# Turning dequantised weights on TensorE: transpose and separate low-rank sum, or identity product with accumulation

## The chip, the cores and the metric

One NeuronCore of a Trainium2 chip runs the whole program. The metric is the device time of one execution in microseconds. The kernel before has a median of 907.61 us in three runs (907.22 to 911.1).

## The reference, cut to what matters

Two post-norm layers over 4 sequences of 512 tokens, 256 channels. Layer 0 is attention (16 heads, 4 key/value heads, rotary) and a mixture of 8 experts with a shared expert; layer 1 is causal attention and the feed-forward block that the change touches:

```
def dequant4bit(q, scale):
    return (q.astype(jnp.float32) - 7.5) * jnp.repeat(scale, 64, axis=1)
w_up = dequant4bit(w_up_q, w_up_scale).T                      # 256 x 1024
y1 = x1 @ w_up + b_up + x1 @ w_up_lora_a @ w_up_lora_b        # rank 16
x2 = jax.nn.relu(y1)
w_down = dequant4bit(w_down_q, w_down_scale).T                # 1024 x 256
y2 = x2 @ w_down + b_down + x2 @ w_down_lora_a @ w_down_lora_b
```

The kernel folds the low-rank part into the weights: it computes w_up + a_up b_up and w_down + a_down b_down once, in float32, and keeps both in SBUF.

## The kernel before

Each engine has one program in order. Part A is layer 0 up to the shared expert, then a loop runs 23 tiles of 128 tokens through the experts, then part C is layer 1. Part C is driven by a list of steps written out by hand (C_START, C_FIRST and so on). Every engine walks the same list and does its share of each step. A step name is a kind and a number; a plus sign means the next batch; `m` is the next of the 44 row-maximum steps of a batch.

Most steps of TensorE fill one of three PSUM banks ("units"), which go round in the order of the list. `take` waits until the bank used three such steps earlier has been emptied, `filled` waits on the reading engine for TensorE, `consumed` waits until a step's bank has been read.

The steps that matter, all in C_START, with the line of their TensorE part:

- Wb, Wat0 to Wat2 (L608): biases and the low-rank "a" factors are transposed; VectorE copies them out (ua_t, da_t).
- Wu0 to Wu3 (L608): four 128x128 transposes of the dequantised up weight each. ScalarE copies the bank to w_up (L978).
- Wul0 to Wul3 (L616): one product of the 16 rows of ua_t with 512 columns of n_ub. VectorE adds the bank to w_up (L1326).
- Wd0 to Wd3 and Wdl0 to Wdl3 (L608, L616): the same for the down weight, with two products of 256 columns. ScalarE copies (L981), VectorE adds (L1330).
- Wq, Wo (L608): transposes of the layer-1 projections, copied by ScalarE.
- cL0, cL1 (L1335 and the lines after L1065): VectorE adds the gathered expert rows and normalises half a batch each. GpSimd gathers the rows by indirect DMA (L1439), for batch 0 before everything else of part C, for batch b+1 after cL1 of batch b.
- cX0, cX1 (L608): transposes of these halves. cQ, cV (L616): projections. cK: VectorE splits queries and keys into three bfloat16 parts, SyncE stores them to DRAM and loads them back stacked.
- m (L830, L832 on TensorE, L1369 on VectorE): scores for the row maxima and their reduction.

The product lines call `nc.tensor.matmul(out, stationary, moving)`; a float32 product shows as two pairs of a weight load and a matmul record, a transpose as one. The weights w_up and w_dn are first used by the cH and cD steps of batch 0, far behind C_START.

Of the kernel before, what the change touches and what calls it, by code (L numbers as in the profile page):

```python
# [25 lines left out]
ALU = mybir.AluOpType  # L26
# [3 lines left out]
P = 128  # L30
B = 4
S = 512
C = 256
# [14 lines left out]
RANK = 16  # L48
# [28 lines left out]
A_LAST = """.V0 -F3 | | -P0 | -P1 | | .F0 | -N0 | -N1 | -R0 | .F1 | | | | .F2 | | |"""  # L77
A_END = """-F3 =Sg0 =Sg1 -P0 =Sg2 =Sg3 =Su0 -P1 =Su1 =Su2 -N0 =Su3 =D0 -N1 -R0 =D1 RK0 -Sg0 -Sg1
-Sg2 -Sg3 -Su0 -Su1 ID0 -Su2 -Su3 -D0 -D1"""
C_START = """Wb0 Wat0 Wat1 Wat2 Wu0 Wul0 Wu1 Wul1 Wu2 Wul2 Wu3 Wul3 cL0 Wq0 Wq1 Wq2 Wo0 Wd0 Wd1 cX0 cL1 Wd2 Wd3 cX1 cQ0 cQ1 cK0 cQ2  # L80
cK1 cQ3 cK2 cV0 cK3 cV1 Wdl0 Wdl1 +cL0 Wdl2 +cX0 +cL1 Wdl3 +cX1 m +cQ0 m +cK0 m m +cQ1 m m m m +cK1 m m
+cQ2 m m m +cK2 m m +cQ3 m m m m +cK3 m m m m m m m m m m m m m m m m m m m m +cV0 m m m m m cM0 +cV1"""
C_FIRST = """+m | | +m +m | +m | +m +m | .cF0 +m +m +m +m | +m +m +m | +m +m +m +m +m | +m +m +m +m | .cF1 +m +m +m | +m +m | +m
+m +m +m +m | +m +m +m | .cF2 +m +m +m +m +m +m +m +m +m | +cM0 >cL0 | >cL1 |"""
# [15 lines left out]
def expand(names, b, m):  # L100

    steps = []
    for x in names.split():
        sign = x[0] if x[0] in "=-.+>" else ""
        to = b + {"=": -2, "-": -1, ".": 0, "+": 1, ">": 2}[sign] if sign else 0
        x = x[len(sign):]
        if x == "m":
            if to < B:
                steps.append(("max", to, m[0]))
            m[0] += 1  # L110
        elif 0 <= to < B:
            kind = x.rstrip("0123456789")
            steps.append((kind, to, int(x[len(kind):])))
    return steps
# [28 lines left out]
def c_order():  # L143

    return (expand(C_START, 0, [0]) + attention_order([C_FIRST, C_SECOND, C_THIRD, C_LAST], "catt")
            + expand(C_END, B, [0]))


def post_ln_layers(nc, ins, out):
# [4 lines left out]
    with ExitStack() as ctx:  # L154
# [23 lines left out]
        ident = place([P])  # L178
# [102 lines left out]
        w_up = place([NC_, HID])  # L281
        w_dn = place([NK, C])
# [5 lines left out]
        n_up = place([NK, C])  # L288
        n_ups = place([NK, C // BLOCK])
        n_dn = place([2, HID])  # L290
        n_dns = place([2, HID // BLOCK])
        n_ua = place([2, RANK])
        n_ub = place([HID])
        n_da = place([NK, RANK])
        n_db = place([C])
        ua_t = place([C])
        da_t = place([HID])
# [119 lines left out]
        def qk_columns(i):  # L417

            return slice(C, QK0) if i == 0 else slice(P * (i - 1), P * i)
# [7 lines left out]
        def take(pe, step):  # L427

            u = unit_no[step]
            if u >= UNITS:  # L430
                pe.wait_ge(unit_free[u % UNITS], u // UNITS)
            return ps[:, 8 - UNITS + u % UNITS, :]

        def filled(eng, step):

            u = unit_no[step]
            eng.wait_ge(unit_full[u % UNITS], u // UNITS + 1)  # L437
            return ps[:, 8 - UNITS + u % UNITS, :]

        def consumed(eng, step):  # L440

            u = unit_no[step]
            eng.wait_ge(unit_free[u % UNITS], u // UNITS + 1)

        def full_of(step):
            return unit_full[unit_no[step] % UNITS]

        def free_of(step):
            return unit_free[unit_no[step] % UNITS]
# [152 lines left out]
        def _(pe):  # L602
            def transposes(step, pieces):

                dst = take(pe, step)
                for col, src, idn, rows in pieces:
                    n = src.shape[0]
                    last = nc.tensor.transpose(dst[0:rows, col:col + n], src, idn)  # L608
                last.then_inc(full_of(step), 1)

            def products(step, groups):

                dst = take(pe, step)
                for (rows, lo, hi), pairs in groups:
                    for n, (a, w) in enumerate(pairs):
                        last = nc.tensor.matmul(dst[0:rows, lo:hi], a, w, start=(n == 0), stop=(n == len(pairs) - 1))  # L616
                last.then_inc(full_of(step), 1)

            def cols(t):
                return slice(P * t, P * (t + 1))  # L620

            pe.wait_ge(s_ident, 16)
            for step in a_steps:
                n, b, i = step
# [15 lines left out]
                elif n == "attS":  # L640
# [5 lines left out]
                    for g in range(4):  # L646
                        if g % 2 == 0 and head0 * b + i:

                            pe.wait_ge(exp_done[g // 2], head0 * b + i)
                        last = nc.tensor.matmul(ps[:, g, :], k_stack[0:STACK, b % 2, hg, cols(kt)],  # L650
                                                q_stack[0:STACK, b % 2, 4 * hg + g, :], start=True, stop=True)
                        if g % 2:
                            last.then_inc(s_full[g // 2], 1)
                elif n == "attP":
# [6 lines left out]
                    for g in range(4):  # L661
                        if g % 2 == 0:
                            pe.wait_ge(exp_done[g // 2], k + 1)
                        last = nc.tensor.matmul(ps[32 * g:32 * g + 32, 4, :], v_aug[:, kt, hg, :],  # L664
                                                (probs0, probs1)[i % 2][:, g, :], start=(kt == 0), stop=(kt == NT - 1))
# [31 lines left out]
                elif n == "ID":  # L697
                    dst = take(pe, step)
                    for t in range(TT):
                        if t % (TT // 2) == 0:  # L700
                            pe.wait_ge(hot_ready, t // (TT // 2) + 1)
                        last = nc.tensor.matmul(dst[:, 0:48], pos_hot[:, t, :], pick[:, t, :], start=(t == 0),
                                                stop=(t == TT - 1))
# [74 lines left out]
            for step in c_steps:  # L778
                n, b, i = step
# [12 lines left out]
                    transposes(step, [(0, n_b[0:4 + NK, :], ident[0:4 + NK, 0:4 + NK], P)])  # L792
                elif n == "Wu":
                    pe.wait_ge(deq, 1)
                    c, half = i // 2, i % 2
                    transposes(step, [(P * r, n_up[:, 4 * half + r, cols(c)], ident, P) for r in range(4)])
                elif n == "Wul":
                    c, half = i // 2, i % 2
                    consumed(pe, ("Wat", 0, 0))
                    products(step, [((P, 0, 512), [(ua_t[0:RANK, cols(c)], n_ub[0:RANK, 512 * half:512 * half + 512])])])  # L800
                elif n == "Wd":
                    pe.wait_ge(deq, 2)
                    transposes(step, [(P * (2 * r + c), n_dn[:, c, cols(2 * i + r)], ident, P)
                                for r in range(2) for c in range(2)])
                elif n == "Wdl":
                    consumed(pe, ("Wat", 0, 2))
                    products(step, [((P, C * r, C * (r + 1)), [(da_t[0:RANK, cols(2 * i + r)], n_db[0:RANK, :])])
                                    for r in range(2)])
                elif n in ("cX", "cN"):
                    pe.wait_ge(x2_ready if n == "cX" else x3_ready, 2 * b + i + 1)  # L810
                    transposes(step, [(P * (2 * t + c), x_sb[:, NT * b + 2 * i + t, cols(c)], ident, P)
# [10 lines left out]
                elif n == "max":  # L822
# [4 lines left out]
                    dst = take(pe, step)  # L827
                    w = P * (qt + 1)
                    for g in range(nh):
                        nc.tensor.matmul(dst[:, w * g:w * (g + 1)], cq_stack[0:STACK, b % 2, h0 + g, cols(qt)],  # L830
                                         ck_stack[0:STACK, b % 2, h0 + g, 0:w], start=True, stop=True)
                        last = nc.tensor.matmul(dst[:, w * g + P * qt:w * (g + 1)], identb, negmask,  # L832
                                                start=False, stop=True, skip_group_check=True)
                    last.then_inc(full_of(step), 1)
                elif n == "cM":
                    pe.wait_ge(m_parts, b + 1)
                    dst = take(pe, step).bitcast(BF16)
                    for t in range(NT):
                        last = nc.tensor.transpose(dst[0:2 * NH, cols(t)], mparts[:, t, :, :].rearrange("p a h -> p (a h)"),
                                                   identb)  # L840
                    last.then_inc(full_of(step), 1)
                elif n == "cattS":
# [6 lines left out]
                    for g in range(4):  # L849
                        h = 4 * hg + g  # L850
                        if g % 2 == 0:

                            pe.wait_ge(exp_done[g // 2], k)
                        last = nc.tensor.matmul(ps[:, g, P * kt:S], ck_stack[0:STACK + 2, b % 2, h, cols(kt)],  # L854
                                                cq_stack[0:STACK + 2, b % 2, h, P * kt:S], start=True, stop=True)
                        if g % 2:
                            last.then_inc(s_full[g // 2], 1)
                elif n == "cattP":
# [7 lines left out]
                    for g in range(4):  # L866
                        last = nc.tensor.matmul(ps[32 * g:32 * g + 32, 4, P * kt:S],  # L867
                                                cv_aug[:, b % 2, kt, 4 * hg + g, :],
                                                cprobs[:, i % 2, g, P * kt:S], start=(kt == 0), stop=(kt == NT - 1))
# [10 lines left out]
                elif n == "cI":  # L880

                    half, k = i // NK, i % NK
# [156 lines left out]
        def _(v):  # L1039
# [72 lines left out]
            for step in a_steps:  # L1112
                n, b, i = step
# [3 lines left out]
                elif n == "rp":  # L1117
# [12 lines left out]
                    r = rot[:, :, qk_columns(i)].rearrange("p t (d h) -> p t d h", d=HD)  # L1130
# [42 lines left out]
                elif n == "R":  # L1173
# [3 lines left out]
                    for t in range(NT):  # L1177
                        last = nc.vector.max(top8[:, t, :], logits[:, t, :])
# [131 lines left out]
            for step in c_steps:  # L1310
                n, b, i = step
                if n == "Wat":
                    dst = ua_t if i == 0 else da_t[:, 512 * (i - 1):512 * i]
                    w = C if i == 0 else 512
                    nc.vector.tensor_copy(dst[0:RANK, :], filled(v, step)[0:RANK, 0:w]).then_inc(free_of(step), 1)
                elif n == "Wb":
# [2 lines left out]
                    nc.vector.tensor_copy(b_qk, src[:, 0:4]).then_inc(free_of(step), 1)  # L1319
                    consumed(v, step)  # L1320
                    nc.vector.tensor_scalar(b_qk[:, 0:2], b_qk[:, 0:2], 0.25, None, ALU.mult).then_inc(bqk_ready, 1)
                elif n == "Wul":
                    c, half = i // 2, i % 2
                    consumed(v, ("Wu", 0, i))
                    dst = w_up[:, c, 512 * half:512 * half + 512]
                    nc.vector.tensor_tensor(dst, filled(v, step), dst, ALU.add).then_inc(free_of(step), 1)  # L1326
                elif n == "Wdl":
                    consumed(v, ("Wd", 0, i))
                    dst = w_dn[:, 2 * i:2 * i + 2, :].rearrange("p r n -> p (r n)")
                    nc.vector.tensor_tensor(dst, filled(v, step), dst, ALU.add).then_inc(free_of(step), 1)  # L1330
                elif n == "cL":

                    rows = x_sb[:, NT * b + 2 * i:NT * b + 2 * i + 2, :]
# [14 lines left out]
                elif n == "cV":  # L1348
# [5 lines left out]
                    for t in range(2):  # L1354
                        last = nc.vector.tensor_tensor(cv_aug[:, b % 2, 2 * i + t, :, 0:HD], src[:, t, :, :],
                                                       bv_b.rearrange("p (h d) -> p h d", d=HD), ALU.add)
# [31 lines left out]
                elif (n == "cH" and i < 2) or (n == "cI" and i % NK == 0):  # L1388

                    half = i if n == "cH" else i // NK  # L1390
# [131 lines left out]
```

## Time and profile before

| | us |
|---|---|
| median of three runs | 907.61 |
| lowest, highest | 907.22, 911.1 |
| the profiled execution | 910.58 |
| its span, first to last instruction | 908.5 |
| TensorE busy | 798.4 |
| VectorE busy | 490.1 |
| ScalarE busy | 367.3 |
| GpSimd busy | 98.5 |

The mean granted TensorE clock over the span is 0.936 of full speed. "Busy" of TensorE is time with a matmul record open, so it includes the tail of each. PE in a row is TensorE's matmul queue, PEld its weight loads, DVE VectorE, ACT ScalarE, POOL GpSimd. Times in a timeline are from the start of the span; the expert loop ends near 455 us and the attention of layer 1 starts at 551.65 us.

### The profile page before, as it was taken

What the parts mean: (1) busy time and instruction counts of PE and PEld (TensorE: products, weight loads), DVE (VectorE), ACT (ScalarE), POOL (GpSimd) and SP (SyncE); (2) the same over time, 40 slices, a digit from 0 to 9 for tenths busy, and PEclk for the clock granted to TensorE, in tenths of its full rate; (3) what the DMA queues carried; (4) which work ended last, traced back from release to release, by engine and by line L of the source; (5) the groups of instructions that cost most, each with busy time, mean ns of one, the idle gap of its engine ahead of it and who ended that gap; (6) DMA issues with size and microseconds to landing.
All of it is one profiled execution on the core that took longest, in us unless ns stands there. A gap on an engine that the chain in (4) does not pass through costs nothing. (4 is left out here: it accounts for less than half of the span.)

```text
span 908.5 us, 11697 instructions
## 1 busy us (share of the span) xinstructions
PE 798.4 (88%) x3907; PEld 419.0 (46%) x3908; DVE 490.1 (54%) x1369; ACT 367.3 (40%) x581; POOL 98.5 (11%) x111
## 2 busy tenths in 40 slices
PE   5599999999998899999987778878998889979886
PEld 3222435344345456666653333434464445533665
DVE  2743852763645522222265794888665955664363
ACT  3388785875842011111142205534423532146130
POOL 0000000000000111111811101221011101012000
PEclk9699999999999999999978798978999979889999
DMA  6558025024061061111117580007200450000000
GB/s 203 152 189 277 10 85 160 1 82 117 24 205 50 18 183 42 45 46 46 29 49 220 148 234 4 1 25 210 68 1 2 129 173 1 2 1 24 12 12 24
DMA packets 51582, 75.02 MB, mean 83 GB/s; under 512 B 7606, under 2 KB 44762, under 8 KB 49226
## 3 DMA queue, kind: packets, MB, share of 16 engines
q1 hardware_dynamic: 49660, 69.26, 25.3%
q0 software_dynamic: 1872, 5.11, 2.2%
q8 instruction: 29, 0.48, 0.2%
q14 instruction: 21, 0.17, 0.1%
HBM read 46.57 MB, written 27.66 MB: 82 GB/s over the span
## 5 line engine op out<-in xcount | busy, mean ns | idle before, releaser
L616 PE MATMUL ps<-arena 128*128 128x256 f32 (+5 forms) x1084 | 340.8, 464 | 22.4 <-DVE arena L1203 5.0
L616 PEld LDWEIGHTS ps<-arena 128*128 128x128 f32 (+1 forms) x1084 | 206.7, 201 | 118.5 <-issue 75.6
L921 ACT ACTIVATE arena<-ps 128x1024 f32<-128x1024 f32 x128 | 124.2, 1027 | 32.8 <-PE ps L650 32.6
L1016 ACT ACTIVATE arena<-ps 128x1024 f32<-128x1024 f32 (+3 forms) x128 | 83.2, 705 | 94.2 <-PE ps L854 93.9
L1369 DVE TENSOR_REDUCE arena<-ps 128x1 f32<-128x512 f32 (+3 forms) x176 | 101.1, 635 | 35.8 <-PE ps L832 31.8
L721 PE MATMUL ps<-arena 128*128 x184 | 88.0, 602 | 1.2 <-DVE arena L1274 1.2
L830 PE MATMUL ps<-arena 96*128 96x128 bf16 (+3 forms) x256 | 66.4, 316 | 14.6 <-DVE arena L1369 9.4
L608 PE MATMUL ps<-arena 128*128 128x128 f32 (+3 forms) x237 | 42.0, 320 | 41.2 <-DVE arena L1086 17.1
L650 PE MATMUL ps<-arena 96*128 96x512 bf16 x256 | 71.5, 391 | 6.7 <-DMA arena<-q_stacks_dram 3.6
L1456 POOL TENSOR_SCALAR_AFFINE_SELECT arena<-arena 128x512 f32<-128x512 f32 x64 | 43.1, 675 | 286.4 <-ACT arena L1016 286.1
L664 PE MATMUL ps<-arena 128*32 128x512 f32 x512 | 69.7, 612 | 2.9 <-DVE arena L1148 2.7
L1415 POOL DMA_INDIRECT arena<-xs_dram,arena x23 | 21.9, 954 | 409.9 <-DVE arena L1268 303.8
L949 ACT ACTIVATE arena<-ps 128x512 f32<-128x512 f32 x23 | 13.8, 598 | 125.7 <-PE ps L721 125.7
L608 PEld LDWEIGHTS ps<-arena 128*128 128x128 f32 (+3 forms) x237 | 32.6, 161 | 56.0 <-issue 19.9
L854 PE MATMUL ps<-arena 98*128 98x512 bf16 (+3 forms) x256 | 50.1, 315 | 8.0 <-ACT arena L1016 4.8
L650 PEld LDWEIGHTS ps<-arena 96*128 96x128 bf16 x256 | 17.9, 98 | 82.5 <-ACT arena L921 40.7
L867 PE MATMUL ps<-arena 128*32 128x128 f32 (+3 forms) x512 | 50.8, 470 | 0.4 <-POOL arena L1456 0.4
L832 PE MATMUL ps<-arena 128*128 128x128 bf16 x256 | 50.7, 227 | 0.0
L830 PEld LDWEIGHTS ps<-arena 96*128 96x128 bf16 x256 | 25.5, 100 | 47.8 <-DVE arena L1369 31.6
L721 PEld LDWEIGHTS ps<-arena 128*128 128x128 f32 x184 | 33.7, 194 | 26.1 <-issue 25.0
L1095 DVE STREAM_TRANSPOSE arena<-arena 128x512 f32<-128x512 f32 x32 | 22.6, 706 | 41.2 <-ACT arena L928 21.2
L738 PE MATMUL ps<-arena 128*128 x184 | 43.6, 380 | 0.8 <-ACT arena L955 0.8
(144 smaller groups left out, 723.7 us busy)
## 6 DMA issues: line engine op xcount, KB each, us to landing
arena<-stacks_dram SPq DMA_DIRECT2D x16, 768.0 KB, 6.3
arena<-in_gate_up_proj SPq DMA_DIRECT2D x8, 1024.0 KB, 9.5
arena<-q_stacks_dram SPq DMA_DIRECT2D x8, 768.0 KB, 5.9
stacks_dram<-arena SPq DMA_DIRECT2D x16, 384.0 KB, 3.3
arena<-in_down_proj SPq DMA_DIRECT2D x8, 512.0 KB, 8.7
stacks_dram<-arena SPq DMA_DIRECT2D x16, 256.0 KB, 3.6
q_stacks_dram<-arena SPq DMA_DIRECT2D x8, 384.0 KB, 4.1
yg_dram<-arena SPq DMA_DIRECT2D x23, 128.0 KB, 1.7
```

Of the source, the lines that this page charges most:

```text
L608: last = nc.tensor.transpose(dst[0:rows, col:col + n], src, idn)
L616: last = nc.tensor.matmul(dst[0:rows, lo:hi], a, w, start=(n == 0), stop=(n == len(pairs) - 1))
L650: last = nc.tensor.matmul(ps[:, g, :], k_stack[0:STACK, b % 2, hg, cols(kt)], q_stack[0:STACK, b % 2, 4 * hg + g, :], start=True, stop=True)
L664: last = nc.tensor.matmul(ps[32 * g:32 * g + 32, 4, :], v_aug[:, kt, hg, :], (probs0, probs1)[i % 2][:, g, :], start=(kt == 0), stop=(kt = ...
L721: last = nc.tensor.matmul(ps[:, 2 * half + up, :], xg_t[:, half, c, :], gu[:, e, c, FE * up:FE * (up + 1)], start=(c == 0), stop=(c == 1))
L830: nc.tensor.matmul(dst[:, w * g:w * (g + 1)], cq_stack[0:STACK, b % 2, h0 + g, cols(qt)], ck_stack[0:STACK, b % 2, h0 + g, 0:w], start=Tru ...
L832: last = nc.tensor.matmul(dst[:, w * g + P * qt:w * (g + 1)], identb, negmask, start=False, stop=True, skip_group_check=True)
L854: last = nc.tensor.matmul(ps[:, g, P * kt:S], ck_stack[0:STACK + 2, b % 2, h, cols(kt)], cq_stack[0:STACK + 2, b % 2, h, P * kt:S], start= ...
L867: last = nc.tensor.matmul(ps[32 * g:32 * g + 32, 4, P * kt:S], cv_aug[:, b % 2, kt, 4 * hg + g, :], cprobs[:, i % 2, g, P * kt:S], start=( ...
L921: nc.scalar.activation(probs[:, 2 * p:2 * p + 2, :], ps[:, 2 * p:2 * p + 2, :], ACT.Exp)\
L1016: nc.scalar.activation(cprobs[:, i % 2, 2 * p:2 * p + 2, P * kt:S], ps[:, 2 * p:2 * p + 2, P * kt:S], ACT.Exp).then_inc(exp_done[p], 1)
L1369: nc.vector.tensor_reduce(mneg[:, qt, h0:h0 + nh], filled(v, step)[:, 0:nh * w].rearrange("p (h n) -> p h n", n=w), AX.X, ALU.max, negate= ...
```

## The change

For each 128x128 tile of the up and down weights, the transpose becomes an ordinary product with the identity as the moving operand, with the tile as stationary operand as before. Directly behind it the low-rank product for the same 128 columns is accumulated onto the same PSUM columns. ScalarE then copies the finished bank. The steps Wul and Wdl are gone from the list and from both engines. The list is reordered: cL0 comes directly behind Wat2; Wq, Wo, Wu0, Wu1 follow; Wu2 stands between cX0 and cX1 of batch 0; Wu3 and Wd0 behind cV1; Wd1 and Wd2 ahead of cX0 of batch 1 and Wd3 between its cX0 and cX1.

```diff
-C_START = """Wb0 Wat0 Wat1 Wat2 Wu0 Wul0 Wu1 Wul1 Wu2 Wul2 Wu3 Wul3 cL0 Wq0 Wq1 Wq2 Wo0 Wd0 Wd1 cX0 cL1 Wd2 Wd3 cX1 cQ0 cQ1 cK0 cQ2
-cK1 cQ3 cK2 cV0 cK3 cV1 Wdl0 Wdl1 +cL0 Wdl2 +cX0 +cL1 Wdl3 +cX1 m +cQ0 m +cK0 m m +cQ1 m m m m +cK1 m m
+C_START = """Wb0 Wat0 Wat1 Wat2 cL0 Wq0 Wq1 Wq2 Wo0 Wu0 Wu1 cX0 cL1 Wu2 cX1 cQ0 cQ1 cK0 cQ2
+cK1 cQ3 cK2 cV0 cK3 cV1 Wu3 Wd0 +cL0 Wd1 Wd2 +cX0 +cL1 Wd3 +cX1 m +cQ0 m +cK0 m m +cQ1 m m m m +cK1 m m
...
                 elif n == "Wu":
                     pe.wait_ge(deq, 1)
+                    consumed(pe, ("Wat", 0, 0))
                     c, half = i // 2, i % 2
-                    transposes(step, [(P * r, n_up[:, 4 * half + r, cols(c)], ident, P) for r in range(4)])
-                elif n == "Wul":
-                    c, half = i // 2, i % 2
-                    consumed(pe, ("Wat", 0, 0))
-                    products(step, [((P, 0, 512), [(ua_t[0:RANK, cols(c)], n_ub[0:RANK, 512 * half:512 * half + 512])])])
+                    dst = take(pe, step)
+                    for r in range(4):
+                        nc.tensor.matmul(dst[:, cols(r)], n_up[:, 4 * half + r, cols(c)], ident, start=True, stop=True)
+                        last = nc.tensor.matmul(dst[:, cols(r)], ua_t[0:RANK, cols(c)], n_ub[0:RANK, cols(4 * half + r)],
+                                                start=False, stop=True, skip_group_check=True)
+                    last.then_inc(full_of(step), 1)
                 elif n == "Wd":
                     pe.wait_ge(deq, 2)
-                    transposes(step, [(P * (2 * r + c), n_dn[:, c, cols(2 * i + r)], ident, P)
-                                for r in range(2) for c in range(2)])
-                elif n == "Wdl":
+                    consumed(pe, ("Wat", 0, 1))
                     consumed(pe, ("Wat", 0, 2))
-                    products(step, [((P, C * r, C * (r + 1)), [(da_t[0:RANK, cols(2 * i + r)], n_db[0:RANK, :])])
-                                    for r in range(2)])
+                    dst = take(pe, step)
+                    for r in range(2):
+                        for c in range(2):
+                            nc.tensor.matmul(dst[:, cols(2 * r + c)], n_dn[:, c, cols(2 * i + r)], ident, start=True,
+                                             stop=True)
+                            last = nc.tensor.matmul(dst[:, cols(2 * r + c)], da_t[0:RANK, cols(2 * i + r)],
+                                                    n_db[0:RANK, cols(c)], start=False, stop=True, skip_group_check=True)
+                    last.then_inc(full_of(step), 1)
...
-                elif n == "Wul":
-                    c, half = i // 2, i % 2
-                    consumed(v, ("Wu", 0, i))
-                    dst = w_up[:, c, 512 * half:512 * half + 512]
-                    nc.vector.tensor_tensor(dst, filled(v, step), dst, ALU.add).then_inc(free_of(step), 1)
-                elif n == "Wdl":
-                    consumed(v, ("Wd", 0, i))
-                    dst = w_dn[:, 2 * i:2 * i + 2, :].rearrange("p r n -> p (r n)")
-                    nc.vector.tensor_tensor(dst, filled(v, step), dst, ALU.add).then_inc(free_of(step), 1)
```

## Rows read from the trace of the kernel before

**Rows 1.** The page, busy time: us, share of span, instructions.

```profile
PE 798.4 (88%) x3907; PEld 419.0 (46%) x3908; DVE 490.1 (54%) x1369; ACT 367.3 (40%) x581; POOL 98.5 (11%) x111
```

**Rows 2.** Stretches: busy us (records) by engine, granted clock, DMA share, GB/s.

```profile
core 0: us, PE busy (x) PEld busy (x) DVE busy (x) ACT busy (x) POOL busy (x), PEclk, DMA share, GB/s
456.00:460.00 4.00, 4.00 (x22) 2.05 (x19) 2.52 (x6) 1.20 (x2) 1.65 (x2) 1.00 0.51 158
460.00:464.00 4.00, 4.00 (x12) 1.93 (x12) 1.39 (x2) 0.80 (x2) 2.24 (x3) 0.59 0.39 113
464.00:468.00 4.00, 4.00 (x13) 2.50 (x13) 2.06 (x5) 3.19 (x5) 0.00 (x0) 0.50 0.02 8
468.00:472.00 4.00, 3.79 (x22) 3.39 (x21) 3.60 (x17) 2.71 (x6) 0.00 (x0) 0.63 0.00 0
...
492.00:496.00 4.00, 2.57 (x10) 1.95 (x11) 3.86 (x9) 0.00 (x0) 0.00 (x0) 0.85 0.98 242
496.00:500.00 4.00, 1.43 (x4) 0.61 (x2) 3.76 (x14) 0.00 (x0) 0.00 (x0) 0.50 1.04 356
...
508.00:512.00 4.00, 4.00 (x15) 2.26 (x14) 0.74 (x2) 0.60 (x1) 3.09 (x4) 0.51 0.32 84
...
530.00:540.00 10.00, 8.09 (x53) 4.16 (x54) 10.00 (x19) 0.00 (x0) 0.00 (x0) 0.83 0.99 288
```

**Rows 3.** Timeline, GpSimd and VectorE, 461 to 476: start, us, what.

```profile
461.91 0.94 POOL L1439 DMA_INDIRECT arena<-yg_dram,arena  x1 [0.31 <-issue]
...
465.87 0.69 DVE L1326 TENSOR_TENSOR arena<-ps,arena 128x512 f32<-128x512 f32 x1 [2.35 <-PE ps L616]
466.48 0.68 DVE L1335 TENSOR_TENSOR arena<-arena 128x512 f32<-128x512 f32 x1
...
475.66 0.41 DVE L1086 TENSOR_SCALAR arena<-arena 128x256 f32<-128x256 f32 x1
```

**Rows 4.** Timeline of TensorE, 458 to 478.

```profile
458.43 0.66 PE L608 MATMUL ps<-arena 128*128 128x128 f32 x4
...
459.02 1.12 PE L616 MATMUL ps<-arena 16*128 16x512 f32 x2
...
460.07 0.66 PE L608 MATMUL ps<-arena 128*128 128x128 f32 x4
...
462.64 1.11 PE L608 MATMUL ps<-arena 128*128 128x128 f32 x4
...
463.69 2.07 PE L616 MATMUL ps<-arena 16*128 16x512 f32 x2
...
465.69 5.38 PE L608 MATMUL ps<-arena 128*128 128x128 f32 x24
...
471.28 1.53 PE L608 MATMUL ps<-arena 128*128 128x128 f32 x12 [0.21 <-DVE arena L1086]
...
476.12 0.66 PE L608 MATMUL ps<-arena 128*128 128x128 f32 x4 [3.31 <-DVE arena L1086]
...
477.51 10.53 PE L616 MATMUL ps<-arena 128*128 128x512 f32 x24 [0.73 <-ACT arena L993]
```

**Rows 5.** Timeline of TensorE and VectorE, 492 to 510.

```profile
492.11 1.96 PE L616 MATMUL ps<-arena 16*128 16x256 f32 x8 [0.58 <-ACT arena L1006]
...
495.87 1.29 DVE L1330 TENSOR_TENSOR arena<-ps,arena 128x512 f32<-128x512 f32 x2
497.08 0.68 DVE L1335 TENSOR_TENSOR arena<-arena 128x512 f32<-128x512 f32 x1
...
501.88 1.11 PE L608 MATMUL ps<-arena 128*128 128x128 f32 x4 [4.45 <-DVE arena L1086]
...
507.32 1.12 PE L608 MATMUL ps<-arena 128*128 128x128 f32 x4 [2.32 <-DVE arena L1086]
...
509.32 0.69 DVE L1369 TENSOR_REDUCE arena<-ps 128x4 f32<-128x512 f32 x1 [1.28 <-PE ps L832]
```

## The prediction

> **What bounds the kernel now.** I read the page first: TensorE is busy 88% of the span and VectorE 54% [rows 1]. A share says nothing about this change, since its steps all stand between the last expert tile (455 us) and the first score matmuls of layer 1 (551 us). So I took the table of stretches [rows 2], then the timelines. From 530 to 540 us VectorE is busy 10.00 of 10.00 us with the row maxima, whatever TensorE does; what counts is when that run of maxima can start. It starts behind cX1 of batch 1, which TensorE begins at 507.32 us and whose first maximum follows at 509.32 [rows 5]. The question is therefore what moves these 507.32 us. Two chains lead there, one behind the other.
>
> First chain: VectorE adds the fourth Wul at 465.87, starts cL0 at 466.48, and cL0 and cL1 end at 476.07 [rows 3]. cX1 of batch 0 starts then, at 476.12, and the first cQ at 477.51 [rows 4]. Here VectorE is last and TensorE waits for it. Everything up to cV1 hangs on the first cQ through the part splitting and its stores to DRAM.
>
> Second chain: after cV1, VectorE adds Wdl0 and Wdl1 (495.87), begins cL0 of batch 1 at 497.08, lets cX0 go at 501.88, adds Wdl2, does cL1, lets cX1 go at 507.32 [rows 5]. TensorE has little to do meanwhile: 1.43 of the 4.00 us from 496 on, and that at the low clock [rows 2].
>
> **What the change removes.** Eight adds of about 0.69 us on VectorE and the eight products Wul, Wdl with their banks. In the first chain cL0 no longer stands behind Wul3's add, but it needs the four gathers; the last is issued at 461.91 [rows 3] and DMA traffic has died out at 464 (0.39 busy before, 0.02 after) [rows 2], so cL0 could start at about 464.7: 1.8 us earlier. In the second chain cL0 of batch 1 starts at 495.85 in place of 497.08 (1.23), and cL1 follows without Wdl2's add (0.65): 1.9 us. On VectorE alone the change is worth 1.8+1.9 = 3.7 us. The extra ScalarE evacuations are none: it copied the eight turned tiles before too, and now does it in stretches where it is idle. SyncE and GpSimd issue the same things in the same order; the waits on the turned low-rank tiles, which Wu and Wd now hold, are met before 458 us, well ahead of any of these steps.
>
> **What it adds to TensorE.** A transpose leaves one record, a float32 product two (Wul: x2 for one product) [rows 4]. The price of a record of 128 columns: twelve transposes take 1.53 us and four 0.66, so 0.109 us at the high clock; twenty-four take 5.38 and four 1.11, so 0.2135 us at the low clock [rows 4]. 512 columns are four times that (0.436 and 0.854), and the row count doesn't matter: eight 16-row records of 256 columns need 1.96 us, as 8 x 0.218 and the tail of the last say [rows 5].
>
> Each new step has four pieces, a 128-row product with the identity and a 16-row product, two records of 128 columns each. Columns alone make that 4 x 0.109 = 0.44 us a piece at the high clock and 0.85 at the low one. But a piece goes from 128 stationary rows to 16 and back, and the trace prices that. Between the starts of Wu2 and Wu1 lie 460.07-458.43 = 1.64 us, with 4 x 0.109 + 2 x 0.436 = 1.31 us of columns: 0.33 us for one change to 16 rows and one back. At the low clock it is 465.69-462.64 = 3.05 against 2.56: 0.49 us [rows 4]. In the run of twenty-four transposes, with step borders and bank waits in it but no change of rows, no such time is lost: its 0.2135 us is just twice 0.109. So a piece costs 0.44+0.33 = 0.77 us (high) or 0.85+0.49 = 1.34 us (low), a step 3.1 or 5.4 us, in place of 0.44 or 0.85 for its transposes. Bounds: 0.44/0.85 if the pause belonged to something else in those steps; 0.88/1.37 if each product ran quite alone (one record plus the tail that four transposes show: 0.66-3x0.109 = 0.33, 1.11-3x0.2135 = 0.47, twice). I take the measured middle.
>
> The Trainium skill says the same from its side: TensorEngine Tiling (Array Packing), Key Properties, has changing the tiling mode (not just the tile) drain TensorE. The rows above show such a cost, 0.17 us a change at the high clock; without it the sum would be a gain.
>
> **The clock.** From 456 to 460 the granted clock is 1.00; then, with TensorE busy all the time in four transposes, a 16-row product, four transposes and so on, it falls to 0.50 and stays there through 464-468 [rows 2]. It comes back only in the unbroken run of transposes (0.63 in 468-472). It falls again at about 494.8 (0.85 over 492-496), in the 16-row work and the idleness after it, and is low until 512 (0.51 in 508-512) [rows 2]. The new steps are that same alternation: 0.22 us of 128-row work in 0.77, where Wu and Wul had 0.44 in 1.64. So I expect the high clock (2.4 GHz) to be lost in them within a few us, and the low one (1.2 GHz) to stay until unbroken 128-row work comes.
>
> **First chain, new.** The transposes up to Wo are done by about 458.7. Wu0 and Wu1 take 6.2 us (high) to 10.8 (low): done at 464.9 to 469.5, and cX0 is due at 471.28-1.8 = 469.5. Covered, just. TensorE has been idle or in the mixture, so the clock is low: cX0 0.85, Wu2 5.4, and cX1 starts at 475.7 where VectorE would allow 474.3. That is 0.4 us before today's; four low-clock transposes cost the same 0.4 more than today's. The first cQ ran almost wholly at the low clock today and will again. Net 0. Bounds: -3.5 (Wu2 hidden at the high clock, -1.8, and the first cQ's four records at 0.436 instead of 0.854, -1.7) to +1 (cX0 late too).
>
> **Second chain, new.** Wu3 starts at 492.1, when ScalarE has freed the bank, as Wdl0 does today [rows 5]. Then Wu3, Wd0, Wd1 and Wd2 stand ahead of cX0, and Wd3 ahead of cX1. Until the clock falls at 494.8, 3.5 pieces; the other 12.5 cost 1.34 each, 16.8: 511.6. cX0 0.85: 512.4. Wd3 5.4: cX1 starts at 517.8, against 507.3: 10.5 us late. VectorE, whose chain would have allowed 505.4, waits. With the fall at 492.1 all sixteen pieces are slow: 21.4, cX1 at 519.8, +12.5. With it at 498.3 it is +8.1. In another execution the fall may come somewhat later than in this one, so I take +9.8. If it never falls: 16 x 0.77 = 12.3, cX0 at 504.4, cX1 at 508.0: +0.7. Without the pauses cX1 is bound by VectorE: -1.9.
>
> Behind cX1 the maxima run as before, VectorE-bound, so nothing gives the time back. Wdl3's add at 507.35 falls into VectorE's wait for the first maximum and is worth nothing.
>
> **Sum.** 0 + 9.8. The traced execution took 910.58 us (span 908.5 and 2.1 around it); it would become 920.4. The median of the runs is 907.61, so the same difference gives 917.4 us.
>
> **Rivals.** (a) No pause: the 0.33 and 0.49 us come from waits on banks in Wu and Wul, not from the change of rows. Then a step is 1.7 or 3.4 us, the clock may hold, and both chains are VectorE's again: -1.8-1.9 = -3.7: 903.9 us, and with the first cQ at the high clock 902.2. Against it: the pause is the same at several borders whose banks were free. This rival ends on the other side; it decides where a piece costs under about 0.53 us (four steps in the 8.5 us from 492.1 to 500.6). (b) The pauses are there but the clock holds: first chain -1.8 to -3.5, second +0.7: -1 to -3, 905.5 us. (c) More than I sum: the fall comes at once, Wu1 delays cX0 too, each change costs the upper bound: 12.5+1 = 13.5: 921 us.
>
> A rule that would turn it: the Trainium skill, TensorE: Matmul & The Clock Gate, Part 4, says that transpose mode does not count as TensorE being busy, so that the full clock does not engage. By it, plain products instead of transposes would lift the clock, and case (b) would be the outcome, 905.5 us. This trace speaks against it: the clock rose during twenty-four transposes and nothing else [rows 2, 4].
>
> **How the numbers follow.** Forecast 0.68, (a) 0.12, (b) 0.08, (c) 0.12. The forecast's own range is 914.5 to 919.5 (+7 to +12). The range to (b) and up to (c) holds about 0.85: 906 to 921.5. Half a per cent, 4.5 us, is about what a measurement of this kernel tells from none. Slower by more: forecast and (c), 0.79. Within: (b) and most of (a), 0.17. Faster by more: the best of (a), 0.04.
>
> **What would show it.** Right: pieces of about 1.3 us apart in Wd0 to Wd3, a granted clock of 0.50 from about 495 to beyond 515, cX1 of batch 1 near 517, cX1 of batch 0 within 1 us of 476, VectorE idle for over 10 us before the first maximum, and all later stages merely shifted. Wrong: a piece under 0.6 us, or a clock of 1.00 in the stretch; then VectorE, not TensorE, releases cX1.

## The result: 12 us slower, in the steps behind cV1

The changed kernel takes 920.33 us in the median of four runs (918.63 to 921.86), against 908.41 of the kernel before in the same comparison (907.22 to 911.1): ratio 1.0127, 95% interval 1.0096 to 1.0157. The forecast was 917.4 us within 906.0 to 921.5, slower by more than half a per cent with a chance of 0.79. The narrower range of its main case, 914.5 to 919.5, was missed by 0.8 us, as much as the kernel before lies above its 907.61 in this comparison; as a difference, 11.9 us is the upper end of its +7 to +12.

The profiled execution took 921.86 us with a span of 919.8. In it the expert loop ended 3.2 us earlier than in the trace of before, which no part of the change explains: in the twelve profiles of this study Wb0, the first transpose of part C, starts anywhere from 452.0 to 455.6 us. So I count everything in part C from Wb0. This row exists once in each trace, first that of before (start us, us, engine, line):

```profile
455.57 0.23 PE L608 MATMUL ps<-arena 12*128 12x12 f32 x1 [0.52 <-DVE arena L1287]
```

and then that of the changed kernel:

```profile
452.40 0.23 PE L608 MATMUL ps<-arena 12*128 12x12 f32 x1 [0.52 <-DVE arena L1293]
```

The stretches of the changed kernel, columns as in [rows 2]: busy us (records), granted clock, DMA share, GB/s.

```profile
456.00:460.00 4.00, 4.00 (x21) 2.86 (x20) 0.00 (x0) 1.18 (x3) 2.84 (x3) 1.00 0.50 137
460.00:464.00 4.00, 2.70 (x12) 1.77 (x11) 2.33 (x10) 0.60 (x1) 0.00 (x0) 0.72 0.11 33
...
468.00:472.00 4.00, 4.00 (x12) 2.76 (x12) 2.76 (x16) 0.05 (x1) 0.65 (x1) 0.50 0.00 0
...
476.00:480.00 4.00, 4.00 (x7) 1.57 (x7) 0.13 (x1) 1.27 (x2) 0.04 (x1) 0.64 0.12 37
...
488.00:492.00 4.00, 3.40 (x18) 2.25 (x16) 3.86 (x9) 1.27 (x2) 0.00 (x0) 1.00 0.97 250
492.00:496.00 4.00, 4.00 (x14) 2.76 (x13) 3.76 (x14) 0.60 (x1) 0.00 (x0) 0.56 1.01 315
...
508.00:512.00 4.00, 4.00 (x15) 2.88 (x14) 0.00 (x0) 1.02 (x2) 0.00 (x0) 0.50 0.11 33
...
516.00:520.00 4.00, 4.00 (x18) 2.85 (x18) 0.69 (x1) 1.19 (x2) 0.00 (x0) 0.50 0.00 0
```

TensorE is busy through all of 492 to 520. The clock falls at 492.5 us (0.56 over 492 to 496), lies at 0.50 from then on and comes back at 523.2. Before, it was TensorE that had little to do there. Now it is VectorE, which does nothing from the end of cL1 to 519.06: the two engines have changed places. The timeline of the changed kernel's TensorE (L799 and L810 are the identity products of Wu and Wd, L800 and L812 their low-rank products):

```profile
472.83 1.11 PE L608 MATMUL ps<-arena 128*128 128x128 f32 x4
474.68 10.90 PE L616 MATMUL ps<-arena 128*128 128x512 f32 x24 [0.73 <-issue]
...
489.52 0.46 PE L799 MATMUL ps<-arena 128*128 128x128 f32 x2 [0.60 <-ACT arena L1012]
...
490.32 0.49 PE L799 MATMUL ps<-arena 128*128 128x128 f32 x2
490.74 0.48 PE L800 MATMUL ps<-arena 16*128 16x128 f32 x2
491.15 0.49 PE L799 MATMUL ps<-arena 128*128 128x128 f32 x2
...
493.78 0.79 PE L812 MATMUL ps<-arena 16*128 16x128 f32 x2
494.51 0.80 PE L810 MATMUL ps<-arena 128*128 128x128 f32 x2
495.23 0.79 PE L812 MATMUL ps<-arena 16*128 16x128 f32 x2
...
510.42 1.11 PE L608 MATMUL ps<-arena 128*128 128x128 f32 x4
...
516.95 1.11 PE L608 MATMUL ps<-arena 128*128 128x128 f32 x4
```

A piece takes 491.15-490.32 = 0.83 us at the high clock and 495.23-493.78 = 1.45 at the low one; the sixteen pieces of Wu3, Wd0, Wd1 and Wd2 fill 489.52 to 510.42 without a gap. And VectorE:

```profile
461.50 0.69 DVE L1332 TENSOR_TENSOR arena<-arena 128x512 f32<-128x512 f32 x1 [6.80 <-DMA arena<-yg_dram,arena]
...
493.26 0.69 DVE L1332 TENSOR_TENSOR arena<-arena 128x512 f32<-128x512 f32 x1
...
502.43 0.41 DVE L1092 TENSOR_SCALAR arena<-arena 128x256 f32<-128x256 f32 x1
519.06 0.69 DVE L1366 TENSOR_REDUCE arena<-ps 128x4 f32<-128x512 f32 x1 [16.22 <-PE ps L838]
```

cL0 of batch 0 now waits for the gathers alone. After cL1 of batch 1 VectorE waits 16.22 us for the first maximum. Counted from Wb0:

| event | before | changed | difference |
|---|---|---|---|
| cL0 of batch 0 starts | 10.9 | 9.1 | -1.8 |
| cX1 of batch 0 starts | 20.6 | 20.4 | -0.1 |
| first cQ starts | 21.9 | 22.3 | +0.3 |
| Wdl0, Wu3 starts | 36.5 | 37.1 | +0.6 |
| cX1 of batch 1 starts | 51.8 | 64.6 | +12.8 |
| first maximum | 53.8 | 66.7 | +12.9 |
| end of the span | 452.9 | 467.4 | +14.5 |

Of these 14.5 us, 12.2 arise between Wu3 and cX1 of batch 1. 1.6 come after the first maximum, where the two programs are the same. That is no more than scatter: in the other ten profiles the time from the first maximum to the end differs from that of before by -1.8 to +2.7 us. With the 3.2 us of the expert loop off, the spans differ by 11.3, the medians by 11.9.

### The profile page after: what moved, and what is told of

The parts are those of the page before. It is cut to its first block and busy times, and to the rows that moved or that the text cites. A ratio compares the mean times of both kernels' runs of the same rounds, so it can differ in the third digit from the quotient of the medians.

```text
span 919.8 us, 11822 instructions
## 1 busy us (share of the span) xinstructions
PE 818.8 (89%) x3979; PEld 435.4 (47%) x3980; DVE 484.9 (53%) x1361; ACT 367.3 (40%) x581; POOL 98.4 (11%) x111
## 5 line engine op out<-in xcount | busy, mean ns | idle before, releaser
L616 PE MATMUL ps<-arena 128*128 128x256 f32 (+3 forms) x1060 | 326.3, 457 | 20.0 <-DVE arena L1209 4.9
L616 PEld LDWEIGHTS ps<-arena 128*128 128x128 f32 x1060 | 199.9, 198 | 112.7 <-issue 73.1
L721 PE MATMUL ps<-arena 128*128 x184 | 86.5, 594 | 1.2 <-DVE arena L1280 1.2
L608 PE MATMUL ps<-arena 128*128 128x128 f32 (+3 forms) x205 | 35.8, 313 | 34.2 <-DVE arena L1147 10.5
L1412 POOL DMA_INDIRECT arena<-xs_dram,arena x23 | 21.9, 951 | 406.8 <-DVE arena L1274 302.0
L838 PE MATMUL ps<-arena 128*128 128x128 bf16 x256 | 51.8, 232 | 0.0
L608 PEld LDWEIGHTS ps<-arena 128*128 128x128 f32 (+3 forms) x205 | 27.0, 156 | 43.8 <-issue 16.2
L721 PEld LDWEIGHTS ps<-arena 128*128 128x128 f32 x184 | 33.1, 190 | 25.3 <-issue 24.2
L860 PEld LDWEIGHTS ps<-arena 98*128 98x128 bf16 x256 | 18.7, 101 | 55.1 <-issue 31.8
```

The source lines that it names most:

```text
L721: last = nc.tensor.matmul(ps[:, 2 * half + up, :], xg_t[:, half, c, :], gu[:, e, c, FE * up:FE * (up + 1)], start=(c == 0), stop=(c == 1))
```

## Experiments

Theory A: the price is the change between 128 and 16 stationary rows, eight times a step, directly and through the clock that falls in it. Rival B: it is the second record of the identity product or the accumulation. Rival C: the clock falls there whatever TensorE does. Rival D: it is the places of the steps.

**The same products with full rows.** The low-rank operands get 112 rows of zeros by four more DMAs among the early loads:

```diff
+                             (n_ub[RANK:P], ins["zeros"]), (n_db[RANK:P], ins["zeros"][:, 0:C]),
+                             (ua_t[RANK:P], ins["zeros"][:, 0:C]), (da_t[RANK:P], ins["zeros"])):
...
-                        last = nc.tensor.matmul(dst[:, cols(r)], ua_t[0:RANK, cols(c)], n_ub[0:RANK, cols(4 * half + r)],
+                        last = nc.tensor.matmul(dst[:, cols(r)], ua_t[0:ROWS, cols(c)], n_ub[0:ROWS, cols(4 * half + r)],
```

(the same for the down weight; ROWS is P).

> Low-rank operands padded with zero rows to 128, so that every record of the new steps has 128 stationary rows; same products, same order, same columns. Theory A (the price is the change between 128 and 16 rows, and through it the clock): a piece costs 4 x 0.109 = 0.44 us at the high clock, the clock stays at 1.00 in the stretch behind cV1, VectorE again releases cX1 of batch 1, both VectorE gains appear: 3 to 4.5 us below the kernel before, 904 to 906. Rival B (the price is the doubled records of the identity product or the accumulation onto a written bank): pieces stay at 0.83 and 1.45 us and the time at 920.

Measured: 903.24 us against 906.97, ratio 0.9954 (0.9938 to 0.9970), so 3.7 us below, as expected. TensorE of this kernel, and VectorE's first maximum:

```profile
489.44 0.39 PE L813 MATMUL ps<-arena 128*128 128x128 f32 x2
489.66 0.39 PE L815 MATMUL ps<-arena 128*128 128x128 f32 x2
489.89 0.39 PE L813 MATMUL ps<-arena 128*128 128x128 f32 x2
...
495.65 0.66 PE L611 MATMUL ps<-arena 128*128 128x128 f32 x4 [1.13 <-DVE arena L1095]
...
500.49 0.95 PE L611 MATMUL ps<-arena 128*128 128x128 f32 x4 [2.39 <-DVE arena L1095]
...
502.44 0.69 DVE L1369 TENSOR_REDUCE arena<-ps 128x4 f32<-128x512 f32 x1 [2.00 <-PE ps L841]
```

A piece is 489.89-489.44 = 0.45 us, and VectorE (L1095) releases both cX steps of batch 1. The first maximum comes 49.0 us behind Wb0 (453.47), 4.8 before that of the kernel before. As many records, as many columns, the same accumulation, the same list: rivals B and D fall, since the whole loss of 12 us has gone and both VectorE gains stand in its place. The clock is 1.00 over 484 to 500 here. And it is the change of rows that pauses, not the small product by itself: eight 16-row records in a row take no more than their columns, 1.96 us [rows 5].

**64 and 96 rows.** The padded kernel with ROWS at 64 and 96.

> As the kernel with low-rank operands padded to 128 rows, but the product uses 64 of them. Theory A1 (a change between any two array modes costs): 64 rows are another mode than 128, so the pauses of 0.09 us and more are back, pieces about 0.8 us at the high clock; half-filled rows keep the clock high longer than 16 did; 908 to 918. Rival A2 (only a very small row count costs): pieces 0.44, 903 to 905.

> The same with 96 of the padded rows. The row-maximum products of 96 rows alternate with 128-row ones in every run here 0.058 us apart at 128 columns of bfloat16, without a pause. Theory A1: 96 rows count as the full array, no pause, pieces 0.44, 903 to 905. Rival A3 (any difference in the row count costs): pieces 0.8 and 908 to 918.

With 96 rows: 905.17 us against 908.15, ratio 0.9959 (0.9936 to 0.9982), pieces of 0.44 us:

```profile
491.27 0.39 PE L803 MATMUL ps<-arena 96*128 96x128 f32 x2
491.49 0.39 PE L802 MATMUL ps<-arena 128*128 128x128 f32 x2
491.71 0.39 PE L803 MATMUL ps<-arena 96*128 96x128 f32 x2
```

With 64: the median is 909.99, ratio 1.0018 (0.9996 to 1.0040), but the eleven runs lie in two groups, eight at 905.36 to 911.0 and three at 918.2, 919.25 and 920.37. The mean granted clock over the span is 0.947 in each of the eight and 0.937 or 0.938 in the three. On the row count both first theories hold: 96 rows go with 128, 64 pay like 16. I looked at the two groups with two more profiles.

> The 64-row kernel once more, for one profile: its eleven runs lay in two groups, 905 to 911 and 918 to 920, and its first profile, of an execution of 918.2 us, showed a granted clock of 0.50 from 492 to 520. Theory A: the pauses are fixed and the clock is what differs; an execution of 905 to 911 shows 1.00 through most of that stretch with the same 0.42 us per product, one of 918 shows 0.50 again. Rival F: the two groups differ elsewhere, and the stretch looks the same in both.

> The same again, in case the other repetition falls into the group that is already profiled: 905 to 911 with the clock at 1.00 through most of 492 to 510, or 918 with 0.50.

They took 918.15 and 912.28 us; the kernel before took 913.05 in its one run beside them. So there are three traces of one and the same program; that of 918.15 us looks like that of 918.2. Stretches of TensorE (busy us, records, clock, DMA share, GB/s) in the execution of 918.2 us, and its first maximum:

```profile
492.00:496.00 4.00, 4.00 (x13) 0.54 1.01 327
...
508.00:512.00 4.00, 4.00 (x15) 0.50 0.11 33
...
518.76 0.69 DVE L1369 TENSOR_REDUCE arena<-ps 128x4 f32<-128x512 f32 x1 [16.09 <-PE ps L841]
```

and in the one of 912.28 us, with two of its pieces:

```profile
492.00:496.00 4.00, 4.00 (x21) 1.00 0.99 289
...
508.00:512.00 4.00, 3.18 (x23) 1.00 0.19 56
...
491.70 0.49 PE L802 MATMUL ps<-arena 128*128 128x128 f32 x2
492.12 0.48 PE L803 MATMUL ps<-arena 64*128 64x128 f32 x2
492.53 0.49 PE L802 MATMUL ps<-arena 128*128 128x128 f32 x2
...
508.36 0.69 DVE L1369 TENSOR_REDUCE arena<-ps 128x4 f32<-128x512 f32 x1 [4.87 <-PE ps L841]
```

Counted from Wb0 (452.21 and 453.05) Wu3 starts at 37.1 and at 37.0 us, so up to there the two agree, and the first maximum comes at 66.6 and at 55.3. In the kernel before it came at 53.8. From Wu3 to the first maximum the padded kernel, which has no pauses, needs 15.3 us, this execution 18.3 and the other 29.5. So behind Wu3 the pauses at the high clock cost 3.0 us and the fall of the clock another 11.2. At the end of the span 6.7 of these 11.2 us are left (463.9 against 457.2 from Wb0). Rival F falls. This is the cleanest separation of the study: one program, the same pauses, and the clock as what differs in that stretch. It also shows that the pauses do not always bring the clock down. What does is not settled: no run here separates the pauses from the few rows.

**The identity product twice.** The second overwrites the first:

```diff
+                        nc.tensor.matmul(dst[:, cols(r)], n_up[:, 4 * half + r, cols(c)], ident, start=True, stop=True)
                         nc.tensor.matmul(dst[:, cols(r)], n_up[:, 4 * half + r, cols(c)], ident, start=True, stop=True)
```

> The changed kernel with each identity product issued twice (the second overwrites the first with the same values), so more TensorE work in the same places. Theory A, its clock part: more of the piece is 128-row work, the clock stays high in the stretch behind cV1, a piece costs 6 x 0.109 + 0.4 = 1.05 us instead of 1.45, sixteen of them 16.8 us instead of about 22: 4 to 7 us FASTER than the changed kernel, about 914 to 916. Rival C (the clock falls there whatever TensorE does, or does not matter): each low-clock piece grows by 0.43 us to 1.87, twenty pieces, about 8 us slower: 928.

916.68 us against 906.97, ratio 1.0114 (1.0097 to 1.0131). The profiled execution does what theory A says:

```profile
492.32 0.49 PE L799 MATMUL ps<-arena 128*128 128x128 f32 x2
492.64 0.39 PE L800 MATMUL ps<-arena 128*128 128x128 f32 x2
492.96 0.48 PE L801 MATMUL ps<-arena 16*128 16x128 f32 x2
493.37 0.49 PE L799 MATMUL ps<-arena 128*128 128x128 f32 x2
...
496.00:500.00 4.00, 4.00 (x24) 1.00 0.99 343
```

More work, but the clock is 1.00 from 488 to 520, a piece takes 1.05 us instead of 1.45, and the first maximum is 62.0 us behind Wb0 where the changed kernel has 66.7. Rival C, which wanted 928, falls: none of the four executions took more than 917.01, and the padded kernel kept its clock there too. But the medians differ by less than I expected: 9.7 us over before against 11.9, and the intervals of the ratios overlap. That adding work makes it faster is clear in the profile only, not in the medians; the profiled execution was the fastest of four (914.83), that of the changed kernel the slowest of its four (921.86).

**The low-rank product first, then the four identity products.** Two changes of rows a step instead of eight:

```diff
+                    nc.tensor.matmul(dst[:, 0:512], ua_t[0:ROWS, cols(c)], n_ub[0:ROWS, 512 * half:512 * half + 512],
+                                     start=True, stop=False, skip_group_check=True)
                     for r in range(4):
-                        nc.tensor.matmul(dst[:, cols(r)], n_up[:, 4 * half + r, cols(c)], ident, start=True, stop=True)
...
+                        last = nc.tensor.matmul(dst[:, cols(r)], n_up[:, 4 * half + r, cols(c)], ident, start=False,
+                                                stop=True, skip_group_check=True)
```

> 16 rows kept, but a step does the low-rank product first (one of 512 columns, or two of 256) and then accumulates the four identity products: two changes of rows in a step instead of eight. Theory A: a step costs 2 x 0.436 + 8 x 0.109 + 0.4 = 2.1 us at the high clock in place of 3.3, half of it in 128-row work, so the clock may hold; if it holds 904 to 907, if it falls (4.0 us a step in place of 5.8) about 911. Rival B: as many records of the identity product and the same accumulation, so 3.3 and 5.8 us a step and 920.

905.58 us against 906.97, ratio 0.9983 (0.9966 to 1.0001): as fast as the kernel before.

```profile
488.85 1.16 PE L802 MATMUL ps<-arena 128*128 128x128 f32 x8
489.94 1.12 PE L811 MATMUL ps<-arena 16*128 16x256 f32 x4
491.00 1.81 PE L815 MATMUL ps<-arena 128*128 128x128 f32 x8
...
494.73 2.08 PE L815 MATMUL ps<-arena 128*128 128x128 f32 x8
496.74 2.07 PE L811 MATMUL ps<-arena 16*128 16x256 f32 x4
498.74 2.08 PE L815 MATMUL ps<-arena 128*128 128x128 f32 x8
```

A step costs 491.00-488.85 = 2.15 us at the high clock and 498.74-494.73 = 4.0 at the low one, as expected, and not rival B's 3.3 and 5.8. In this execution (906.74 us) the clock fell at 491.3 all the same and came back near 501.5. I had expected 911 us for a fall, so that part was too high: the first maximum still comes 50.7 us behind Wb0, 3.0 before that of the kernel before.

**A transpose in place of the identity product**, the low-rank product accumulated behind it as in the changed kernel:

```diff
-                        nc.tensor.matmul(dst[:, cols(r)], n_up[:, 4 * half + r, cols(c)], ident, start=True, stop=True)
+                        nc.tensor.transpose(dst[:, cols(r)], n_up[:, 4 * half + r, cols(c)], ident)
```

> The changed kernel with the identity product put back to a transpose (one record) and the low-rank product accumulated behind it as before; eight changes of rows a step stay. Theory A: a piece loses one record, 0.83 to 0.72 us and 1.45 to 1.23; the clock still falls; twenty low-clock pieces save 0.21 each, 4 us: about 916. Rival B (the identity product's second record is the price): back to about 905 to 908.

912.27 us against 906.97, ratio 1.0074 (1.0046 to 1.0103): better than the 916 of theory A, far from rival B's 905 to 908. The low-rank products of two neighbouring pieces:

```profile
494.18 0.79 PE L811 MATMUL ps<-arena 16*128 16x128 f32 x2
...
495.31 0.79 PE L811 MATMUL ps<-arena 16*128 16x128 f32 x2
```

A low-clock piece is 1.13 us, 0.32 less than with the identity product, not the 0.21 of a record's columns. At the high clock it is 0.67 us (489.33 to 490.00), 0.16 less than 0.83 and not 0.11. So the two-record product on the 128-row side of a change pays more than a single transpose there.

**The new list, the old method.** The kernel before with the changed kernel's C_START, in which each Wul and Wdl stands behind its Wu or Wd:

```diff
+C_START = """Wb0 Wat0 Wat1 Wat2 cL0 Wq0 Wq1 Wq2 Wo0 Wu0 Wul0 Wu1 Wul1 cX0 cL1 Wu2 Wul2 cX1 cQ0 cQ1 cK0 cQ2
+cK1 cQ3 cK2 cV0 cK3 cV1 Wu3 Wul3 Wd0 Wdl0 +cL0 Wd1 Wdl1 Wd2 Wdl2 +cX0 +cL1 Wd3 Wdl3 +cX1 m +cQ0 m +cK0 m m +cQ1 m m m m +cK1 m m
```

> The kernel before with the list order of the changed one and nothing else: transposes, separate 16-row products, VectorE adds, each Wul and Wdl directly behind its Wu and Wd. Theory A (what costs is the alternation inside the new steps, not the places): Wu3, Wd0, Wd1, Wd2 with their low-rank products are 4 x 1.65 = 6.6 us at the high clock or 12 at the low one in 8.5 us, so cX1 of batch 1 is 0 to 5 us late and VectorE's adds are all back on its path: 907 to 913, well under the changed kernel. Rival D (moving the steps behind cV1 is what costs, however they are computed): 918 to 921.

909.41 us against 908.15, ratio 1.0025 (1.0003 to 1.0048). The first maximum comes 2.3 us later than in the kernel before, counted from Wb0. So the new places, with two changes of rows a step and VectorE's adds kept, cost 0.3 to 4.4 us by the interval of the ratio, and not 10: rival D falls once more.

**Both cures.** Transposes, and low-rank operands of 128 rows.

> Both cures together: transposes (one record) in place of identity products, and the low-rank product accumulated behind each with operands padded to 128 rows. Theory A: a piece costs 3 x 0.109 = 0.33 us at the high clock, 0.64 at the low one, no pause; VectorE releases both cX steps, so it can win on the padded kernel only where that one met the low clock: 902 to 905, the fastest so far. Rival E (accumulating on a transpose costs a drain of its own): pieces over 0.5 us, 906 to 910.

904.52 us against 908.15, ratio 0.9967 (0.9949 to 0.9986). Two pieces (L802 transposes, L803 low-rank products):

```profile
492.00 0.27 PE L802 MATMUL ps<-arena 128*128 128x128 f32 x1
492.11 0.39 PE L803 MATMUL ps<-arena 128*128 128x128 f32 x2
492.33 0.27 PE L802 MATMUL ps<-arena 128*128 128x128 f32 x1
```

A piece is 0.33 us, its three records and nothing more: rival E falls. But the kernel is not the fastest so far, which I had expected; it can't be told from the padded kernel with identity products. Both leave VectorE as what releases cX1, so the record that it saves is hidden. Both beat the kernel before, by 0.3 to 0.5%.

## Why the prediction was right

The mechanism was right, and so was the place: pauses at each change of rows, the fall of the clock in them, TensorE in VectorE's stead ahead of cX1 of batch 1. The sizes were less good than the time suggests. To the first maximum the loss is 12.9 us where the sum had 9.8: the second chain gave 12.2 where its working had 10.5, of which I had taken off 0.7 for a later fall of the clock that did not come. That cX1 of batch 1 stands at 516.95, "near 517" as forecast, is luck: the expert loop ended 3.2 us earlier, and counted from Wb0 cX1 is 2.3 us later than the 517.8 of the sum. Two slips in the working changed little: a fall at 498.3 gives +7.9 and not +8.1, and the stated range begins at 906.0, just above the 905.5 of the case (b) it was to reach.

- **VectorE's part.** cL0 of batch 0 was to start 1.8 us earlier: it did, 1.8. The gain was to be swallowed by Wu2 at the low clock: cX1 of batch 0 started 0.1 us earlier (0.4 forecast), the first cQ 0.3 later (0 forecast). In the padded kernel Wu2 is shorter and both gains show: cX1 of batch 0 is 1.8 us earlier, and 1.9 are gained behind Wu3. The other 1.1 of its 4.8 us come between, where the 24 records that begin with the first cQ take 8.83 us instead of 10.53, at a better clock.
- **The price of a change of rows.** 0.33 us (high) and 0.49 (low) for two changes, read from the spacing of Wu and Wul [rows 4]. Measured: 0.83-0.44 = 0.39 and 1.45-0.85 = 0.60. This is the mis-sized term. I had priced the change with transposes on the 128-row side; the runs show that a product of two records pays more. With transposes a low-clock piece is 1.13 us, columns 0.64, so 0.49, exactly the figure of the trace before. My upper bound of 1.37 for the low-clock piece was too low by 0.08. Some 16 low-clock pieces, each 0.11 over the 1.34 of the sum, make up the 1.7 us by which the second chain came out longer than the sum for a fall at 494.8 (27.4 us from Wu3 to cX1 of batch 1 instead of 25.7).
- **How the pause lies.** In a high-clock piece of the changed kernel each of the four records starts 0.20 to 0.21 us behind the one before it, where its columns are 0.109: about 0.1 us is lost ahead of the first record behind a change and as much ahead of the second. The Trainium skill (TensorEngine Tiling (Array Packing), Key Properties) has changing the tiling mode drain TensorE. The runs agree: 16 and 64 rows pay, 96 beside 128 do not (0.44 us a piece), and 96 is no smaller array in that page's list of modes (Available Configurations). That the pause is such a drain is the page's account; the runs show only its size.
- **The clock** fell 3.0 us into Wu3 (489.52 to 492.5) and 6.0 us into Wu0 (455.74 to 461.8), and stayed low beyond 520, as the alternation of Wu and Wul had shown in [rows 2]. The rule of the Trainium skill (TensorE: Matmul & The Clock Gate, Part 4), by which plain products in place of transposes would lift it, did not decide here: it fell with plain products only, and with padded rows it was 1.00 over 484 to 500 both with identity products and with transposes.
- **Nothing gives it back** in the changed kernel: the 12.9 us at the first maximum are all still there at the end.

Not settled: what brings the clock down, the few rows or the pauses, and why one program sometimes keeps it; and why the twice-issued identity product gains 4.7 us at the first maximum in its profile and only about 2 in the medians against before.

## What to carry to other kernels

A product with few contraction rows is not cheap because it is small: between full-row products of 128 columns each one cost 0.39 us in pauses at the high clock, almost as much as the columns, and such steps can cost the clock too, which was more (11.2 us against 3.0 behind Wu3 in the 64-row kernel). Group such products, or pad their rows with zeros to 96 or more: in these runs the padded records took no longer than the small ones, and the pauses were gone. And when work moves from another engine to TensorE, price the step at the low clock too, for the new steps may bring the low clock themselves.

## What the runs showed of the hardware

- A change between 128 stationary rows and 16 or 64 costs about 0.2 us at the high clock and 0.3 at the low one in a chain of float32 products (pieces of 0.83 and 1.45 us with two changes, 0.44 and 0.85 of columns); between 128 and 96 nothing (pieces of 0.44).
- One and the same program, with 64-row products alternating with 128-row ones, ran at 905 to 912 us or at 918 to 920. In the three executions with a trace the difference is whether the granted clock held in the 27 us from about 492.4 on.
- A low-rank product of 128 padded rows, accumulated onto a float32 transpose, costs no pause of its own (a piece of 0.33 us is three records of 0.109).
